# An SSM cross layer with a routed feed-forward: scatter waits by token range, the routing weight on VectorE, padding rows not gathered, a third up chunk in single passes

## The reference

```python
aff = sigmoid(x @ wa)                        # 16 experts
p, i = top_k(aff, 2);  p = p / sum(p)
expert(x) = (gelu(x @ g + gb) * (x @ w1 + b1)) @ w2 + b2     # 512 -> 256 -> 512
out = x + sum of 2 shared experts(x) + sum over the 2 chosen experts of p * expert(x)
```

## Time and profile before

| | |
|---|---|
| median of 3 runs | 884.83 us (881.93 to 885.36) |
| the profiled execution | 884.4 us, span 882.3 us |
| granted TensorE clock | 0.96 of full speed over the span |
| TensorE, VectorE, ScalarE, GpSimd busy | 89%, 75%, 63%, 62% |
| DMA busy in the last ten of 40 slices | 0.6, 7, 8, 6, 7, 6, 7, 8, 7, 5, 3 tenths, read from the page |
| gather L599, scatter L631 (two groups) | 1055 ns; 1693 and 1656 ns mean to issue |

### The profile page before, as it was taken

The page is one execution under the profiler, slowest core; times in us unless marked ns, Lnnn a source line. Parts: engine busy times, 40 slices in busy tenths (PEclk is TensorE's granted clock), DMA queues, the critical chain, the costliest instruction groups (busy, mean ns, idle before and its releaser), DMA issues.

```text
span 882.3 us, 16042 instructions
## 1 busy us (share of the span) xinstructions
PE 783.9 (89%) x4358; PEld 589.2 (67%) x4359; DVE 660.8 (75%) x859; ACT 557.5 (63%) x931; POOL 550.5 (62%) x347
## 2 busy tenths in 40 slices
PE   6963799999999988997899999999999998999992
PEld 3622688888888878886777778886555554555551
DVE  4999999999999998999586759544655555556651
ACT  3896899999999999994333431024555554545541
POOL 9651399989999999997815560211444543546532
PEclk9975899999999999999799999999999999999996
DMA  6010311212141122101220121366577867678753
GB/s 182 1 55 0 108 52 58 60 49 61 50 155 49 54 61 92 59 14 49 95 96 1 49 102 42 129 253 275 121 163 226 235 175 223 154 211 205 180 143 48
DMA packets 35384, 95.57 MB, mean 108 GB/s; under 512 B 7760, under 2 KB 8272, under 8 KB 32000
## 3 DMA queue, kind: packets, MB, share of 16 engines
q1 hardware_dynamic: 23360, 65.50, 21.6%
q0 software_dynamic: 11968, 29.37, 15.6%
HBM read 122.24 MB, written 21.36 MB: 163 GB/s over the span
## 4 chain that ended last, share of the span: by engine, by line
PE 43%; DMA 17%; DVE 17%; POOL 9%; issue 7%; ACT 5%; POOLq 1%; DVEq 0%; SPq 0%; ACTq 0%
DVE r L1060 12%; DMA out<-sb_sb,ids 9%; DMA out<-sg,ids 8%; PE ps L1446 6%; PE ps L1448 6%; PE ps L1447 6%; PE ps L1549 5%; POOL r L526 5%; PE ps L1572 5%; PE ps L1550 3%; PE ps L1774 3%; PE ps L1793 2%; DVE r L963 1%; POOL r L599 1%; ACT mem L765 1%
## 5 line engine op out<-in xcount | busy, mean ns | idle before, releaser
L526 POOL TENSOR_TENSOR r<-r,mem 128x1024 f32<-128x1024 f32 x126 | 295.4, 2380 | 34.8 <-DVE r L1060 34.2
L1060 DVE TENSOR_TENSOR_SCAN r<-r,ps 128x1024 f32<-128x1024 f32 x128 | 286.7, 2276 | 9.7 <-issue 9.1
L750 ACT ACTIVATE r<-mem,nega 128x511 f32<-128x511 f32 x256 | 166.9, 714 | 1.8 <-DVE r L1060 1.7
L1549 PE MATMUL ps<-ident,mem 128*128 128x128 f32 x768 | 130.3, 279 | 28.4 <-DVE r L1060 21.7
L1572 PE MATMUL ps<-ident,r 128*128 128x128 f32 x1024 | 132.6, 273 | 1.5 <-POOL r L526 1.3
L765 ACT ACTIVATE mem<-mem,b_turned 128x512 f32<-128x512 f32 x192 | 124.7, 715 | 8.7 <-PE ps L1550 8.3
L1549 PEld LDWEIGHTS ps<-ident,mem 128*128 128x128 f32 x768 | 87.2, 142 | 53.8 <-issue 52.8
L1572 PEld LDWEIGHTS ps<-ident,r 128*128 128x128 f32 x1024 | 115.8, 141 | 2.3 <-POOL r L526 1.8
L1550 PE MATMUL ps<-mem 128*128 128x128 f32 x512 | 99.7, 277 | 0.0
L1793 PE MATMUL ps<-mem 128*128 x188 | 92.2, 615 | 1.8 <-ACT mem L915 1.0
L1446 PE MATMUL ps<-split 128*128 128x512 f32 x216 | 88.2, 408 | 4.8 <-DVE split L1134 2.3
(11 more groups left out here) (205 smaller groups left out, 1304.8 us busy)
## 6 DMA issues: line engine op xcount, KB each, us to landing
r<-in_r_up SPq DMA_DIRECT2D x47, 1024.0 KB
mem<-in_r_down SPq DMA_DIRECT2D x47, 512.0 KB
mem<-cm_rows SPq DMA_DIRECT2D x64, 256.0 KB, 3.3
mem<-in_r_b SPq DMA_DIRECT2D x4, 2048.0 KB, 15.1
out<-acc POOLq DMA_DIRECT2D x17, 256.0 KB, 3.2
r<-in_x SPq DMA_DIRECT2D x4, 1024.0 KB, 4.9
xn_scratch<-r SPq DMA_DIRECT2D x16, 256.0 KB, 2.7
mem<-in_ctx_t SPq DMA_DIRECT2D x4, 512.0 KB, 7.7
```

Source lines behind the costliest of these rows:

```text
L526: pool.tensor_tensor(state[:, k % 2, ec:ec + 2], state[:, k % 2, ec:ec + 2], c, ALU.mult).then_inc(s["weighed"], 1)
L750: act.activation(decay[:, k % 2, ec, 1:L], delta[:, b, ec, 1:L], ACT.Exp, scale=nega[:, ec, n:n + 1]).then_inc(s["decay_ready"], 1)
L1060: dve.tensor_tensor_scan(state[:, half, ec:ec + 2].rearrange("p e l -> p (e l)"), decay[:, half, ec:ec + 2].rearrange("p e l -> p (e l)"), ...
L1549: pe.transpose(ps[:, ec, lt * P:(lt + 1) * P], dbu_t[:, k % 2, lt, ec * P:(ec + 1) * P], ident[:])
```

## The change

`KSPLIT` goes from 2 to 3, and buffers are laid out anew for it; ScalarE then waits for twelve stored tiles instead of eight before its first head. `block_result` on ScalarE goes: the routing weight (one value per row, column j of `row_w`) is multiplied in by VectorE, into the hidden block (`hidden`) and into the bias (`add_bias`), by three-operand instructions; since it is in the hidden block ahead of the down product, the result is the same sum. In VectorE's step `hidden(j)` now stands ahead of `add_bias(j - 2)`. The gather gets a bounds check, so that rows numbered 2048 and up are skipped and the buffer keeps what it held. `blk_wait` is computed from token ranges: row 0 of a block is its first token, row 127 (brought to partition 0 by one small product) its last; a scatter waits for its neighbour where the ranges overlap.

```diff
-KSPLIT = 2
+KSPLIT = 3
...
             def fetch(j):
                 pool.indirect_dma_start(out=xg[:, j % RING], out_offset=None, in_=xn_dram,
-                                        in_offset=bass.IndirectOffsetOnAxis(ids[:, j:j + 1], 0)).then_inc(
+                                        in_offset=bass.IndirectOffsetOnAxis(ids[:, j:j + 1], 0),
+                                        bounds_check=T - 1, oob_is_err=False).then_inc(
                                             s[f"xg_{j % RING}"], 16)
...
-                act.copy(xgt[:, half], ps[:, 4 + half, KSPLIT * P:D]).then_inc(s["xgt_copied"], 1)
+                act.copy(xgt[:, half, 0:D - KSPLIT * P], ps[:, 4 + half, KSPLIT * P:D]).then_inc(s["xgt_copied"], 1)
...
-            def block_result(j, r):
-                act.wait_ge(s["yb_ready"], j + 1)
-                act.activation(y_sb[r], y_sb[r], ACT.Copy, scale=row_w[:, ds(j, 1)]).then_inc(s["y_ready"], 1)
...
-            act.wait_ge(s["early_stored"], 16 * NT // 2)
+            act.wait_ge(s["early_stored"], 16 * (NT - LT))
...
+                dve.wait_ge(s["blocks_ready"], 2)
+                dve.tensor_scalar(row_ids[:], ps[:, SIDE_BANK[0], 0:NBLK], pad_f[:, 0:1], None, ALU.add).then_inc(s["bar_made"], 1)
+            def list_waits():
+                first, last = row_ids[0:1], ps[0:1, 2, F:F + NBLK]
+                dve.wait_ge(s["bar_made"], 1)
+                dve.wait_ge(s["lasts_ready"], 1)
+                dve.tensor_tensor(blk_bar[0:1, 1:NBLK], first[:, 1:NBLK], last[:, 0:NBLK - 1], ALU.is_le).then_inc(s["bar_made"], 1)
+                dve.tensor_tensor(blk_f[0:1, 1:NBLK], first[:, 0:NBLK - 1], last[:, 1:NBLK], ALU.is_le).then_inc(s["bar_made"], 1)
+                dve.wait_ge(s["bar_made"], 3)
+                dve.tensor_tensor(blk_bar[0:1, 1:NBLK], blk_bar[0:1, 1:NBLK], blk_f[0:1, 1:NBLK], ALU.mult).then_inc(s["bar_made"], 1)
+                dve.wait_ge(s["bar_made"], 4)
+                dve.scalar_tensor_tensor(out=blk_wait[0:1, 1:NBLK], in0=blk_bar[0:1, 1:NBLK], scalar=16.0, in1=half_f[0:1, 2:NBLK + 1],
+                                         op0=ALU.mult, op1=ALU.add).then_inc(s["bar_made"], 1)
...
-                dve.tensor_tensor(hy[:, half], hg[:, half], hb[:, half, F:2 * F], ALU.mult).then_inc(s["hy_ready"], 1)
+                dve.scalar_tensor_tensor(out=hy[:, half], in0=hg[:, half], scalar=row_w[:, ds(j, 1)], in1=hb[:, half, F:2 * F],
+                                         op0=ALU.mult, op1=ALU.mult).then_inc(s["hy_ready"], 1)
...
-                dve.tensor_tensor(y_sb[r], ps[:, 6 + r % 2], tile(b2_all, e), ALU.add).then_inc(s["yb_ready"], 1)
+                dve.scalar_tensor_tensor(out=y_sb[r], in0=tile(b2_all, e), scalar=row_w[:, ds(j, 1)], in1=ps[:, 6 + r % 2],
+                                         op0=ALU.mult, op1=ALU.add).then_inc(s["y_ready"], 1)
...
+                hidden(j, r % 2)
                 if not isinstance(j, int) or j >= 4:
                     add_bias(j - 2, (r - 2) % RING, round_ + (r - 2) // RING)
-                hidden(j, r % 2)
...
+            list_waits()
...
+            pe.wait_ge(s["bar_made"], 1)
+            pe.matmul(ps[0:1, 2, F:F + NBLK], ident[:, P - 1:P], row_ids[:], start=True, stop=True).then_inc(s["lasts_ready"], 1)
             up(0, 0)
```

More of the change, by code:

```diff
@@ L221, in bass_xattn_scan_moe_kernel @@
         with ExitStack() as listing:
-            blk_val = listing.enter_context(nc.sbuf_tensor("blk_val", [P, 2, GROUP, 2 * NBLK], F32))
-        blk_val_again = sb("blk_val_again", [P, 2 * GROUP * 2 * NBLK])
+            blk_val_all = listing.enter_context(nc.sbuf_tensor("blk_val", [P, 4 * KSPLIT * P], F32))
+        blk_val_again = sb("blk_val_again", [P, 4 * KSPLIT * P])
+        blk_val = blk_val_all[:, 0:2 * GROUP * 2 * NBLK].rearrange("p (a g j) -> p a g j", a=2, g=GROUP)
         AHEAD_OF_DOWN = (2 * SH * FC, 2 * SH * FC + 1)
-        blk_val_all = blk_val[:].rearrange("p a g j -> p (a g j)")
         def raw_hidden(i):
@@ L232, in raw_hidden @@
             return sy_raw[:, i % (SH * FC)]
-        half_i = sb("half_i", [P, 2 * ((NBLK + 3) // 2)], I32)
+        half_i = row_i[:, 0:2 * ((NBLK + 3) // 2)]
         half_f = sb("half_f", [P, 2 * ((NBLK + 3) // 2)])
@@ L255, in bass_xattn_scan_moe_kernel @@
         blk_run = sb("blk_run", [P, NBLK])
+        row_ids = blk_run
         blk_load = sb("blk_load", [P, NBLK], I32)
@@ L286, in bass_xattn_scan_moe_kernel @@
         uph_made upr_made xgr_made up_0 up_1 up_2 up_3 down_0 down_1 down_2 down_3 xg_0 xg_1 xg_2 xg_3 xgt_ready xgt_copied h_ready
-        hb_ready hg_ready hy_ready hyt_ready hyt_copied o_ready yb_ready y_ready y_even y_odd
+        hb_ready hg_ready hy_ready hyt_ready hyt_copied o_ready lasts_ready y_ready y_even y_odd
         """.split()
@@ L378, in _ @@
                     sp.dma_start(xn_dram[t * P:(t + 1) * P, :], xn[b % 2][:, lt, :]).then_inc(s["xn_odd_stored" if b % 2 else "xn_even_stored"], 16)
-            sp.wait_ge(s["blocks_ready"], 3)
+            sp.wait_ge(s["blocks_ready"], 2)
             sp.wait_ge(s["base_ready"], NT)
@@ L445, in _ @@
             pool.iota(tok_i[:], [[P, NT]], base=0, channel_multiplier=1).then_inc(s["consts_made"], 1)
-            pool.iota(half_i[:], [[16, (NBLK + 3) // 2], [0, 2]], base=-16, channel_multiplier=0).then_inc(s["consts_made"], 1)
             pool.tensor_copy(iota_f[:], row_i[:, 0:48]).then_inc(s["consts_made"], 1)
+            pool.wait_ge(s["consts_made"], 5)
+            pool.iota(half_i, [[16, (NBLK + 3) // 2], [0, 2]], base=-16, channel_multiplier=0).then_inc(s["consts_made"], 1)
             pool.wait_ge(s["consts_made"], 6)
@@ L452, in _ @@
             pool.tensor_copy(tok_f[:], tok_i[:]).then_inc(s["consts_made"], 1)
-            pool.tensor_copy(half_f[:], half_i[:]).then_inc(s["consts_made"], 1)
+            pool.tensor_copy(half_f[:], half_i).then_inc(s["consts_made"], 1)
             pool.wait_ge(s["consts_made"], 8)
@@ L587, in store_base @@
                 pool.wait_ge(s["so_added"], t + 1)
-                pool.dma_start(out[t * P:(t + 1) * P, :], acc[:, t]).then_inc(s["early_stored" if t < NT // 2 else "late_stored"], 16)
+                pool.dma_start(out[t * P:(t + 1) * P, :], acc[:, t]).then_inc(s["early_stored" if t < NT - LT else "late_stored"], 16)
             for t in range(NT - LT):
@@ L619, in _ @@
                 if j == 0:
-                    pool.wait_ge(s["early_stored"], 16 * NT // 2)
-                    pool.wait_ge(s["late_stored"], 16 * NT // 2)
+                    pool.wait_ge(s["early_stored"], 16 * (NT - LT))
+                    pool.wait_ge(s["late_stored"], 16 * LT)
                 pool.wait_ge(s["y_ready"], j + 1)
@@ L627, in _ @@
                 elif j >= 3:
+                    if j == 3:
+                        pool.wait_ge(s["bar_made"], 5)
                     landed = pool.value_load(blk_wait[0:1, j:j + 1], min_val=16, max_val=16 * NBLK)
@@ L926, in step @@
                 hidden_gate(j, r % 2)
-                if not isinstance(j, int) or j >= 4:
-                    block_result(j - 2, (r - 2) % RING)
                 turn_hidden(j, r % 2)
[L930 to L934, removed]
+            act.wait_ge(s["blocks_ready"], 2)
             turn_tokens(0, 0)
@@ L947, in _ @@
                 step(j, j // RING, j % RING)
-            for j in range(NBLK - 2, NBLK):
-                block_result(j, j % RING)
         @block.vector
@@ L1271, in list_blocks @@
                 dve.tensor_copy(blk_load[:], blk_new[:]).then_inc(s["blocks_ready"], 1)
[L1272 to L1277, removed]
                 dve.tensor_tensor_scan(blk_run[:], ones[:, 0:NBLK], blk_new[:], -1.0, ALU.mult, ALU.add).then_inc(s["run_made"], 1)
@@ L1362, in _ @@
                 hidden_rests(i)
-            dve.wait_ge(s["blocks_ready"], 3)
+            dve.wait_ge(s["blocks_ready"], 2)
             def expert_of(j):
@@ L1790, in down @@
                     pe.wait_ge(s["so_added"], NT)
-                since(pe, s["yb_ready"], j - 1)
+                since(pe, s["y_ready"], j - 1)
                 for fc in range(FC):
@@ L1806, in _ @@
             up_shared(15)
-            pe.wait_ge(s["blocks_ready"], 3)
+            pe.wait_ge(s["blocks_ready"], 2)
             pe.wait_ge(s["ids_ready"], 2)
```

## The result

The changed kernel takes 893.13 us (median of 4 runs, 891.61 to 894.29) against 883.99 us (4 runs, 881.93 to 885.36) before: a ratio of 1.013, 95% interval 1.0103 to 1.0157. The forecast was 876, its range 864 to 888. The profiled execution has a span of 891.0 us against 882.3; the granted clock is alike (0.966 and 0.960 of full speed over the span).

The account below looks back on a forecast made before the run. It took TensorE's 5.49 us a block plus 11.7 us of stalls, mainly from late scatters, as the bound. Scatter waits -11.4, weighting -0.8 and the new engine loop +3.9 summed to -8.3, so 876 us; range 864 to 888.

Parts of the forecast that it names:

- The loop, +3.9: ScalarE, VectorE and TensorE wait in a loop of 11.19 us per two blocks, 5.60 a block: +3.9 us over 37 blocks.
- Rival B: VectorE's two hand-overs behind the gelu, 1.35 us each, make the loop 6.01 a block: slower, 892 us; chance 0.18.
- Scatter waits, -11.4: Range comparison lets two scatters be in flight, so TensorE's stalls behind late scatters go: -11.4 us, bounds 0 to 11.4.
- So the ring waits fall away: VectorE's waits for result buffers, reused after four blocks, end as the scatters' 15 us lag disappears: gain 11.4 us.
- What is late next is VectorE: Once scatters are on time, VectorE's place in the ScalarE and TensorE loop sets the pace, 5.60 us a block.
- rival C: Scatters were limited by bandwidth, not waiting; result-buffer waits remain, only 0.8 us gained: 883.6 us; chance 0.10.
- The first eight blocks, 0: The stage's first eight blocks, with unrolled code and smaller gaps, lose nothing to the engine loop: 0 us.
- ScalarE's weighting, -0.8: Weighting moved to VectorE takes a 0.72 us activation and a handover off the path setting the end: -0.8 us.
- The third chunk: Single-pass up products save TensorE 0.155 us a block, -7.3 over 47 blocks, but lengthen ScalarE's heads and VectorE's remainders.
- Padding: Skipping 1920 of 6016 gathered rows thins traffic, but TensorE hardly waits for gathers: 0 us, bounds -1 to +2.
- Rival A: TensorE stays the bound at 5.34 to 5.4 us a block because register work runs ahead: 866 us; chance 0.27.
- the gap is zero after long waits: Argument for TensorE staying the bound: VectorE's issue gap before the weight remainder, half a microsecond, vanishes after long waits.

Follow-up runs that it names:

- e4: Changed kernel, VectorE's two register reads (bias addition's expert, weight remainder's slot) moved ahead of the hidden product: 881.21 us, 1.0002 of the kernel before.
- h4: Changed kernel, VectorE's two register reads moved ahead of the hidden product and SyncE's loop written out: 871.68 us, 0.9886 of the kernel before.
- f1: Changed kernel, loading only the first four experts' weights: 895.77 us, 1.0191 of the kernel before.
- h2: Changed kernel with SyncE's loop over the blocks written out: 894.47 us, 1.0152 of the kernel before.
- e2: Kernel before plus only the scatter waits by token range: 880.76 us, 0.9998 of the kernel before.
- g3: Kernel before plus the scatter waits by token range, with SyncE's loop written out: 873.63 us, 0.9896 of the kernel before.
- h1: Kernel before with only SyncE's loop over the blocks written out: 879.53 us, 0.9974 of the kernel before.
- f4: Kernel before, loading only the first four experts' weights: 873.98 us, 0.9906 of the kernel before.
- g2: Changed kernel, bias addition ahead of the hidden product, VectorE's two register reads ahead of both, SyncE's loop written out: 867.64 us, 0.984 of the kernel before.
- h3: Changed kernel, bias addition first, VectorE's register reads early, SyncE's loop written out, padding gathered again: 868.55 us, 0.9871 of the kernel before.
- e1: Changed kernel with VectorE's bias addition put back ahead of the hidden product: 880.23 us, 1.0004 of the kernel before.
- e3: Changed kernel with `KSPLIT = 2`, buffers as before: 880.69 us, 0.9998 of the kernel before.

## Why the prediction was wrong

The forecast was -8.3 us, and the profiled executions are 8.7 apart the other way, a miss of 17.0. Of these 12.4 lie in the loop of ScalarE, VectorE and TensorE, 2.2 in the first eight blocks and 2.3 behind block 41. The scatter stalls did go, but their term would have been the next to fail.

**The loop, +3.9: the step that failed. Right mechanism, wrong size.** The changed kernel does wait where the prediction said, at 6.0 a block and not 5.60. Term by term, from the turn shown above: copy to the gelu's end 3.42 us for 3.13 (ScalarE's gap ahead of its head is 0.71 in this turn and was 0.40 in the turn of the kernel before that the 3.13 rests on); gelu to hidden product 0.17 for 0.05; hidden to bias addition 1.12 for 0.93; bias to remainder 0.92 for 0.93; 1.68 and 0.60 as said; 0.55 and 0.10 for 0.54 and 0.10; up products to the next copy 3.45 for 3.23. Sum 12.01 for 11.19. Four small terms were off, all to the same side. The 33 blocks take 16.3 us more than 33 times the 5.49 of before, where the prediction had 3.9 for its loop; less the 11.4 of stalls that is the +4.9 measured. e4 and h4 show what made the loop slow: with VectorE's two reads out of it the 33 blocks of h4 come 5.48 us apart on average. f1 and h2 show that neither the weights nor SyncE had a part in it.

**Rival B** (892) was right in sign, place, pace and time. Its cause was right in kind, though it put the whole on the two hand-overs (1.35 each), which measured 1.12 and 0.92; the rest came from ScalarE and TensorE, so that the agreement of the pace is in part luck. It had 0.18. The stated range leaves out more than "the far part of B": B's own time, 892, lies outside its 888.

**Scatter waits, -11.4: gone here, but not worth 11.4.** At 6.0 us a block VectorE hardly waits for scatters (2.7 us), as foretold, and SyncE, which turns a block in about 5.8, keeps up: its up loads go 1.6 to 3.0 us behind the down products all through, where in e2 that grows to 7.2. In a kernel that runs at the forecast's own 5.49 to 5.60 two sentences fail. "So the ring waits fall away": in e2 and g3 VectorE still waits for the padding's scatters, at results 9 to 11 and not only from 13 on. "What is late next is VectorE": SyncE is late next as well. In the kernel before, every scatter stall let it catch up (its lateness falls back to between 0.4 and 2.8 us at the stalls), which is why had only 0.9 us of `in_r_up`. Take the stalls away and it falls behind by 0.3 us a block until the weights are late. By e2 the term was worth nothing as the kernel stood, and by g3 against h1 some 7 us with SyncE out of the way. The bound "0 (scatters limited by bandwidth)" was in the text, rival C, but for another reason; f4 fits C in part: without the weights' traffic the old waits cost no more than the new ones. No run has the new order with the old waits, so what the range waits give there is not shown.

**The first eight blocks, 0:** measured +2.2. One interval is 6.87 instead of 5.76, behind block 2, where VectorE adds two biases in one step of the same loop (at 615.55); all kernels with three chunks show it (6.74 to 6.87), those with two do not (5.76 to 5.78). The last of the eight, 6.47, is the slow loop already.

**ScalarE's weighting, -0.8:** hidden by the loop (from block 41 to the end +1.5). In g2 that stretch is 37.7 us, 1.3 less than before, some 0.6 of it from four blocks of faster products.

**The third chunk:** g2 runs at TensorE's 5.34 and is 6.0 us below g3 (same chip), near the 7.3 reckoned for 47 blocks; the two differ in the rest of the change as well, so this is not the chunk's share alone. **Padding:** price 0, and h3 agrees. The gather's issue is 1.061 us in g2 and 1.079 in h3; over all runs its mean is 0.99 to 1.08 without the bounds check and 1.05 to 1.16 with it, so a cost of the check, if there is one, is under 0.2 us a block and hidden.

Rival A (866), TensorE bound, is what g2 reaches; it needed the reads moved, the bias addition back in front, and SyncE relieved. The argument for A, "the gap is zero after long waits", took the wrong cause from the rows. At 690.08 the long wait stood at the bias addition, ahead of the hidden product, and the gelu had ended at 686.91, so the slot read could pass while the bias addition and the hidden product ran. That is a reading of the order, not a test. But where the hidden product itself waits long, the gap stays: in the changed kernel its waits reach 2.2 us, and e1 shows the same. First the kernel before, then e1:

```profile
689.02 0.69 DVE L1399 TENSOR_TENSOR sb_sb<-ps,mem 128x512 f32<-128x512 f32 x1 [4.33 <-DMA out<-sb_sb,ids]
...
813.30 0.48 DVE L1393 SCALAR_TENSOR_TENSOR mem<-mem,row_w 128x256 f32<-128x256 f32 x1 [2.34 <-ACT mem L914]
814.24 1.76 DVE L1374 TENSOR_TENSOR acc_again<-r,acc_again 128x1536 fp32r<-128x1536 f32 x1 [0.45 <-issue]
```

The Trainium skill ("Advanced Engine Details and Errata", Sequencer Loop) has a control instruction executed by the sequencer, while engine instructions queue and wait by themselves. The traces agree in half: reads placed ahead of the waiting hidden product cost nothing (h4), while reads behind it were not done during its wait of 2.16 us but after it (0.63 us of issue at 837.60).

## What to carry to other kernels

A gap that costs nothing today, because nobody waits behind it, becomes a term of the sum when a new order puts it on a loop: add up the loop with every gap in it, and let the range reach the time of the rival that such a sum gives. Before counting a stall as gain, ask of every queue, the load-issuing one too, whether it could keep the pace without that stall: here SyncE's rows, 5.8 us a block in e2, said no, and the busy shares show nothing of it. Register reads belong ahead of the instruction that waits, not between it and those that follow it on the loop. When two limits stand close together, test them crossed: the two fixes alone gave 0 and 0.3%, together they gave 1%.

## What the runs showed of the hardware

- A load that SyncE issues in a register-counted loop (three register reads, a wait, a conditional transfer) takes it a median of 2.6 to 3.1 us in e2, also when the transfer is skipped. The shortest step from a down load to the next up load fell, with the loop written out, from 2.49 us (skipped) and 2.75 (made) in e2 to 2.26 and 2.51 in g3; the medians there have waits for the engines in them. Whether the address registers or the loop's own instructions make the difference was not separated.
- A conditional transfer mostly shows 0.35 us of issue when it is made and 0.08 to 0.09 when it is skipped.
- GpSimd's scatters take longer to issue in most kernels with the three-chunk remainder on VectorE: means of 1.93 and 1.97 us in the changed kernel, 2.00 and 2.17 in e1, 1.96 and 1.97 in h3, but 1.65 and 1.88 in e4 and 1.74 and 1.90 in h4, against 1.66 and 1.69 before and 1.66 and 1.67 in e3, which differs from the changed kernel in the chunk alone. It cost nothing that these runs show; its cause was not tried.
